# A first routed layer run ahead of the state-space scans instead of behind them, in a two-layer kernel on one core

## The reference

```python
xn = layernorm(x)
x = x + scan_block(xn) + routed_experts(xn)      # layer 0
xn = layernorm(x)
x = x + retention(xn) + two_of_sixteen(xn)       # layer 1

# scan_block: 256 inner channels, N = 16 states
Xm = silu(conv4(Xn @ W_up1));  delta = softplus(Xm @ W_ll + b)
A_bar = exp(delta * A);  U = Xm * (A_bar - 1) / (delta * A) * delta * B
H_t = A_bar_t * H_{t-1} + U_t;  y_t = sum_n C_t[n] * H_t[:, n]
out = X + (y * silu(Xn @ W_up2)) @ W_down

# routed_experts: each of 8 experts takes its 512 best tokens
G, idx = top_k(softmax(xn @ Wr).T, 512)
X_e = gelu(xn[idx] @ W1 + b1) @ W2 + b2
out = zeros.at[idx].add(G * X_e)
```

## Time and profile before

| | us |
|---|---|
| median of three runs | 572.08 |
| profiled execution | 572.04 |
| its span, first to last instruction | 570.2 |
| busy in the span: PE, DVE, ACT, POOL | 502.4, 420.6, 324.8, 370.8 |
| front, to the first scan of batch 0 | 0 to 89.0 |
| scans, to the last residual | 89.0 to 300.1 |
| experts 1 to 7, and the sums of all eight | 300.1 to 372.6 |
| second layer | 372.6 to 570.2 |

### The profile page before, as it was taken

One profiled execution on the slowest core, in us unless ns is written; L12 is line 12 of the kernel. 1 busy time (PEld: TensorE's weight loads), 2 busy tenths in 40 slices (PEclk: granted clock), 3 DMA queues, 4 the chain that ended last, 5 costly groups with the idle time before them and its releaser, 6 DMA issues.

```text
span 570.2 us, 14135 instructions
## 1 busy us (share of the span) xinstructions
PE 502.4 (88%) x4743; PEld 360.6 (63%) x4744; DVE 420.6 (74%) x1031; ACT 324.8 (57%) x787; POOL 370.8 (65%) x335
## 2 busy tenths in 40 slices
PE   0999987689999999999779999987889899999980
PEld 0643445456676777666547766544566899999970
DVE  4556549999999999999974235588767766666664
ACT  1787669567797897896133444146665544444420
POOL 5078676668898999999964776612567245455540
PEclk9899997859999999999899999998899899999995
DMA  8999631322130340414505456698111212222207
GB/s 224 171 240 294 177 113 43 128 96 101 52 151 16 151 159 7 166 23 161 187 21 159 145 181 203 189 337 327 34 48 50 62 47 61 57 54 54 57 9 221
DMA packets 58164, 70.95 MB, mean 124 GB/s; under 512 B 9343, under 2 KB 45270, under 8 KB 55168
## 3 DMA queue, kind: packets, MB, share of 16 engines
q1 hardware_dynamic: 52432, 57.84, 32.3%
q0 software_dynamic: 5392, 11.76, 8.1%
q10 hardware_dynamic: 288, 0.66, 0.5%
HBM read 50.03 MB, written 21.25 MB: 125 GB/s over the span
## 4 chain that ended last, share of the span: by engine, by line
PE 49%; POOL 18%; DVE 16%; ACT 6%; issue 5%; DMA 4%; SPq 1%; DVEq 0%; POOLq 0%; ACTq 0%
POOL arena L2064 14%; PE banks L1627 8%; PE banks L1614 8%; PE banks L1390 5%; PE banks L1250 5%; DVE arena L569 5%; POOL xm L2051 3%; PE banks L1324 3%; PE banks L1164 3%; PE banks L1174 3%; PE banks L1410 2%; PE banks L1467 2%; ACT arena L1744 2%; PE banks L1354 2%; DVE hbuf L769 1%
## 5 line engine op out<-in xcount | busy, mean ns | idle before, releaser
L2064 POOL TENSOR_TENSOR arena<-arena,bd 128x512 f32<-128x512 f32 x125 | 158.1, 1288 | 23.7 <-DVE arena L569 23.0
L569 DVE TENSOR_TENSOR_SCAN arena<-banks,arena 128x256 f32<-128x256 f32 x256 | 156.4, 669 | 3.2 <-PE banks L1164 1.3
L1744 ACT ACTIVATE arena<-delta,nega 128x256 f32<-128x256 f32 x256 | 109.5, 495 | 35.4 <-PE banks L1174 26.9
L2154 POOL DMA_INDIRECT pair_rows<-w1b,xnT x48 | 49.6, 1033 | 58.9 <-DVE w1b L858 51.8
L1627 PE MATMUL banks<-arena,hbuf 128*128 x384 | 54.7, 285 | 0.7 <-issue 0.2
L1614 PE MATMUL banks<-xsT,xm 128*128 128x128 f32 x384 | 51.1, 276 | 0.8 <-DVE acc L832 0.8
L1627 PEld LDWEIGHTS banks<-arena,hbuf 128*128 128x128 f32 x384 | 46.5, 191 | 3.6 <-issue 2.0
L1164 PE MATMUL banks<-xnT,xnw 44*128 44x172 f32 x384 | 39.9, 344 | 8.6 <-DVE arena L569 6.1
L1614 PEld LDWEIGHTS banks<-xsT,xm 128*128 128x128 f32 x384 | 46.6, 192 | 1.2 <-DVE acc L832 1.0
L2102 POOL DMA_INDIRECT expert_rows<-gate,zbuf x32 | 35.4, 1106 | 17.3 <-issue 8.8
L1830 ACT ACTIVATE hbuf<-banks,colv 128x512 f32<-128x512 f32 x32 | 22.0, 688 | 40.4 <-PE banks L1250 39.7
(11 more groups left out here) (312 smaller groups left out, 999.7 us busy)
## 6 DMA issues: line engine op xcount, KB each, us to landing
bd<-c_rows SPq DMA_DIRECT2D x16, 1024.0 KB, 6.4
expert_rows<-blank SPq DMA_DIRECT2D x8, 1024.0 KB, 10.0
xnT<-expert_rows SPq DMA_DIRECT2D x4, 1024.0 KB, 4.9
bd<-in_w SPq DMA_DIRECT2D x4, 1024.0 KB, 12.9
arena<-in_w SPq DMA_DIRECT2D x4, 1024.0 KB, 13.9
slots_in<-blank POOLq DMA_DIRECT2D x1, 3120.0 KB
xnT<-slots_in SPq DMA_DIRECT2D x48, 65.0 KB
xnw<-expert_rows SPq DMA_DIRECT2D x3, 1024.0 KB, 6.2
```

Of the source, the lines that this page charges most:

```text
L569: m = V.tensor_tensor_scan(ring[:, s, r, :], dw_view(s)[:, 2 * (s % 2) + r, :], ring[:, s, r, :], 0.0, ALU.add, ALU.mult)
L1744: m = nc.scalar.activation(ring[:, s, r, :], delta[:, half(s), bass.ds(b * L, L)], ACT.Exp, scale=negs[:, half(s), n:n + 1])
L2064: nc.gpsimd.tensor_tensor(ring[:, s, :, :], ring[:, s, :, :], c_view(par, s), ALU.mult).then_inc(S["z_pool"], 1)
L2154: nc.gpsimd.indirect_dma_start(out=yd, out_offset=bass.IndirectOffsetOnAxis(ap=xs[:, u, P:P + 1].bitcast(I32), axis=0), in_=ys[:, u % 4, : ...
```

## The change

The eight experts run in one piece between the front and the scans. Their buffers move to places that are free then: gathered rows and the transposed rows to `bd` (four experts deep), weights to `xnT` and `w1b`/`w2b` (four deep), the gated output to the upper half of `z2p`, the rows read back to the upper half of `arena` (experts 6 and 7 to the weight buffers). All eight index lists come from one-hots, with the counting row now read from SBUF. Staircases, compaction and gathers leave the batches. The preparation of the first scan batch moves from the front behind the last `up0`, and its bands go from POOL to DVE. All softplus work of ACT and DVE is done ahead of the experts' loop. The rows of experts 6 and 7 are added during batches 1 and 2, a quarter after steps 3, 5, 7 and 9. The second layer starts straight from the last residual, with 6 instead of 20 useless products, and its loads of constants go out during batch 7. Half of x is loaded by ACT, and the convolution weights wait for it.

```diff
 # DVE
-            for c in range(2): add_log(c)          # ahead of place
 def one_hot(e):
-    V.tensor_tensor(hot[e - AHEAD], iota_ps[:, None, :]..., place[:, :, e:e + 1]..., ALU.is_equal)
+    if e > 1: dve.wait_ge(S["cp_ready"], e - 1)
+    V.tensor_tensor(hot[e % 2], iota_p[:, None, :]..., place[:, :, e:e + 1]..., ALU.is_equal)
+one_hot(0); one_hot(1); indices(0); one_hot(2); indices(1)
+for c in range(2): add_log(c)
+indices(2); one_hot(3)
+for c in range(2, 6): add_log(c)
+for k in range(4): last_steps(k)
+dve_at["steps"] = link.n
+for e in range(E0):
+    if e + AHEAD < E0: indices(e + AHEAD)          # AHEAD = 3
+    if e == E0 - 1:
+        for g in range(4): band(0, 0, g)
+    gated(e)
+    if e + AHEAD + 1 < E0: one_hot(e + AHEAD + 1)
+    if e > 1: row_sum(e - 2)
 def main(b, par, last=False):
-    (batch 0: add_log and last_steps; indices at s == 1)
+    if b in (1, 2) and 2 < s < 11 and s % 2:
+        e = E0 - 3 + b
+        if s == 3: dve.wait_ge(S[f"rows_in{e % 2}"], 80); dve.wait_ge(S["dn_evac"], 1 + b)
+        sum_rows(e, (s - 3) // 2)
 for b in range(NB): main(b, b % 2, b == NB - 1)
-one_hot(5); ...; one_hot(7); expert_steps(((3, gated), (5, row_sum))); layer0_sum(q)
 # SP
+for e in range(2): weights(e)
 sp.wait_ge(S["gates_ready"], 1); (gates into token_rows)
+for e in range(2, 4): weights(e)
+sp.wait_ge(S["dve_link"], dve_at["steps"]); (b2r)
+for e in range(4): weights(e + 4); rows_in(e)
+rows_in(4); rows_in(5); c_spread(0)
+rows_in(6); c_spread(1)        # its second half now waits for ye_ready of all eight
+rows_in(7)                     # waits for row_sum 7
 for b in range(2, NB): c_spread(b)
 sp.wait_ge(S["ab_ready"], 7 * 16); (constants of layer 1)
+sp.wait_ge(S["dve_done"], 7); resident(q)
 # PE
-    (in widen, last block: pro1a(0); pro1b(0); pro2(0))
+for e in range(AHEAD): compact(e)
+turn_rows(0)
+for e in range(E0):
+    if 0 < e < E0 - 1: down0(e - 1)
+    up0(e)
+    if e + AHEAD < E0: compact(e + AHEAD)
+    if e + 1 < E0: turn_rows(e + 1)
+pro1a(0); pro1b(0); down0(E0 - 2); pro2(0); down0(E0 - 1)
 fill(0, 0, 0); fill(0, 0, 1); pro3(0)
 for b in range(NB): main(b, b % 2, b < NB - 1)
-keep_busy(12, 4 * P); pe.wait_ge(S["pair_in0"], 16); keep_busy(8, 4 * P)
+pe.wait_ge(S["dn_evac"], 10); keep_busy(6, 4 * P)
 # ACT
+for q in range(1, 4, 2): act.dma_start(acc[quarter q], x[quarter q])
+act.dma_start(wup1, w_up1); act.wait_ge(S["rows_at1"], 16); (convb)
+logarithms((6, 7)); rows_out(0); expert_steps(((2, gelus), (1, rows_out)))
+act.wait_ge(S["cp_ready"], E0); pro_a(0, 0)
 def main(b, par, more):
+    if b == 0 and s == 8: act.wait_ge(S["row_sum"], E0 - 2)
-    (stair; size_parts, size_exps and logarithms in batch 0)
 # POOL
 def gather(e, q):
+    if e > 3: pool.wait_ge(S["ye_ready"], e - 3)
-    (in main: band of batch 0, gather at chosen steps)
+for e in range(E0):
+    for q in range(4): gather(e, q)
+    if e >= AHEAD: put(e - AHEAD)
+for e in range(E0 - AHEAD, E0):
+    if e == E0 - 1: pro_c(0)
+    put(e)
+for b in range(NB): main(b, b % 2, b < NB - 1)
```

More of the change, by code:

```diff
@@ new lines, in _ @@
+            one_hot(0)
+            one_hot(1)
+            indices(0)
+            one_hot(2)
+            indices(1)
+            for c in range(2):
+                add_log(c)
+            indices(2)
+            one_hot(3)
+            for c in range(2, 6):
+                add_log(c)
+            for k in range(4):
+                last_steps(k)
+                dve.wait_ge(S["dve_link"], link.n)
+            dve_at["steps"] = link.n
+            for e in range(E0):
+                if e + AHEAD < E0:
+                    indices(e + AHEAD)
+                if e == E0 - 1:
+                    for g in range(4):
+                        band(0, 0, g)
+                gated(e)
+                if e + AHEAD + 1 < E0:
+                    one_hot(e + AHEAD + 1)
+                if e > 1:
+                    row_sum(e - 2)
@@ L1253, in main, with down0 @@
+            def down0(e):
+                pe.wait_ge(S["h_ready"], (e + 1) * HC)
+                if e > 1:
+                    pe.wait_ge(S["ye_ready"], e - 1)
+                for q in range(4):
+                    for c in range(HC):
+                        m = pe.matmul(bank[4 + e % 2][:, q * P:(q + 1) * P], hbuf[:, e % 2, c, q * P:(q + 1) * P],
+                                      w2e[e][:, c, :], start=(c == 0), stop=(c == HC - 1))
+                m.then_inc(S["d_ready"], 1)
             def main(b, par, more):
@@ L1739, in main @@
                     act.wait_ge(S["y_done"], b * 8 + (2 * (s // 4) + s % 2 + 1))
-                    if not later(b, 1) and s == 10:
-                        act.wait_ge(S["dve_link"], dve_at["logs"])
+                    if b == 0 and s == 8:
+                        act.wait_ge(S["row_sum"], E0 - 2)
                     for r in range(2):
@@ L1836, in rows_out @@
                     act.wait_ge(S["u_ready"], (e - 1) * HC)
-                nc.scalar.activation(xgT[:, e % 2, :], bank[6 if e else 7][:, :], ACT.Copy).then_inc(S["xg_sb"], 1)
+                nc.scalar.activation(xgT[:, e % 2, :], bank[6][:, :], ACT.Copy).then_inc(S["xg_sb"], 1)
             rows_out(0)
             expert_steps(((2, gelus), (1, rows_out)))
+            act.wait_ge(S["cp_ready"], E0)
+            pro_a(0, 0)
+            act.wait_ge(S["dve_link"], dve_at["steps"])
+            for b in range(NB):
+                main(b, b % 2, b < NB - 1)
             def third_norm(q):
```

449 lines of the change are left out of this document (163 added, 286 removed).

## The result

The changed kernel took **579.36 us** (median of 20 runs, 574.06 to 583.21), the kernel before 574.54 (20 runs on the same chips, 571.31 to 580.92). The ratio is **1.0079, 95% interval 1.0051 to 1.0106**: slower by 0.5 to 1.1%. The profiled execution took 577.68 us, 575.8 of it span, against 572.04 and 570.2; that pair differs by 5.6 us, a little more than the medians (4.8).

A forecast was written before the change was run, and what follows sets the result against it. DVE was taken to pace the batches, with the experts a PE pipeline behind them. Experts and front reach the first scan at 188.0; scans 190.7, seam 3.5, then 5.6, 190.6 and 1.84 give 580.2 us; range 574 to 587.

The forecast's parts named there:

- seam: Between scans and second layer: half the last sum, finish, down, residual and handovers take 3.5 us; before it was 10.
- the rest: From the second layer's first transposition to the end of the span: stays at 190.6 us.
- Blocking: In the experts: POOL's indirect copies wait for the end of one-hots with two SBUF inputs, 3.9 and 6.8 us.
- The first rival: In the experts: one-hots do not block POOL's copies, 3.9 and 5.8 us go, 570.5 us, no change; chance 0.23.
- POOL ends last in the experts: At the last gathered rows: POOL, not PE, ends last by 5.8 us; without the blocking, even with PE.
- DVE sets the pace of the scans: In the scan batches: DVE, not POOL, is the bound; batches 3 to 6 take 91.1 us.
- The second rival: In the scans: POOL is the bound, so leaving gathers save 22 us instead of about 5: 563 us; chance 0.07.
- Row sums: In batches 1 and 2: four DVE additions of expert rows each, at 0.85 us, 3.4 us per batch.
- Batch 7: Last scan batch: 27.22 us less an index list, a wait and 2.1 of three slowed products, 24.0 us.
- The front: From the start to `tokp`: 88.95 us falls by 4.8 to 84.15.
- The load of x: At the start: half of x on the other queue lets DVE start earlier, 1.3 us less (bounds 0 and 2.5).
- The third rival: In the experts: PE's clock falls in pauses waiting for the last gathers, costing 5 us: 586 us; chance 0.14.

The follow-up runs named there:

- counter_psum: The changed kernel with the eight one-hots reading their counter from PSUM instead of SBUF; ratio to the kernel before 0.9938, median 571.15 us.
- before_counter_sbuf: The kernel before with the counter of its three DVE one-hots in SBUF instead of PSUM, nothing else; one execution, 572.85 us.
- sums_on_pool: The changed kernel with the eight row sums of experts 6 and 7 on POOL, in batches 1, 2, 4 and 5; ratio to the kernel before 0.9953.

## Why the prediction was right

The direction and the mechanism held, and the sum missed the profiled execution by 2.5 us and the median (579.36) by 0.8. Its steps, with what the trace has in their place:

| step | predicted | measured |
|---|---|---|
| `tokp` | 84.15 | 82.83 |
| `tokp` to first gather | 5.05 | 5.67 |
| first gather to first transposition | 11.2 | 9.09 |
| fourth index list | 110.3 | 105.6 |
| PE's wait for the last rows | 5.8 | 5.64 |
| last transposition ends | 167.2 | 163.3 |
| first scan of batch 0 | 188.0 | 184.69 |
| scans | 190.7 | 188.68 |
| seam | 3.5 | 3.97 |
| to the first transposition of the second layer | 5.6 | 5.89 |
| the rest | 190.6 | 192.57 |

That the time came so near is in part luck. Up to the end of the scans the trace is 5.3 us ahead of the sum, because most steps were priced too dear; 2.8 us come back behind that, 2.0 of them with the 16 products at the lower clock level. And the sum counts from an execution of 572.04, while the kernel before took 574.54 in the twenty runs beside the changed one. The change itself was forecast at 8.2 us and measured at 4.8 (medians) or 5.6 (the profiled pair). Its ratio, 1.0079, lies within the 1% that the prediction set as the bound of "same", to which it gave 0.29; only by the time, 579.36 against a bound of 577.8, is it "slower".

**Blocking** (the cost that the diff does not show) is what decided it. The steps priced it at 3.9 + 6.8 = 10.7 us on POOL; the long copies show 2.6 + 5.9 = 8.4, and `counter_psum` took it away with one operand: ratio 1.0079 to 0.9938. The first rival (no blocking) is out by that. The forecast puts 9.7 us between itself and that rival; `counter_psum` shows 6.0 of the way, and 8.2 between the medians. So the term was somewhat too dear, and that the rival's 570.5 is nearly the time of the kernel with the cause removed (571.15 the median, 572.13 the profiled execution) owes something to the other steps. The size was taken from rows of 1.25 and 1.49 us beside operations of 1.35 and 2.49. These are two rows with the delay, not the three that the prediction counts, and the copy does not end when DVE ends: the first ends 0.86 us behind the product (291.53 against 290.67), as the six do behind the one-hots. The first miss of the term is `one_hot(2)`, which began 0.95 us ahead of the first gather instead of together with it, and so cost 1.35 and not 2.2.

The Trainium skill, "SBUF — State Buffer", section "Who interferes with whom", had a sentence for each side. The trace agrees with the first (a DVE instruction with two SBUF inputs holds up a GpSimd instruction that reads SBUF, for its whole length): copies of 2.88 and 2.95 us behind one-hots that began 0.25 and 0.18 earlier. The second, that a `tensor_tensor` was not seen to stall the writing of descriptors, gives no safety here, since these one-hots are `tensor_tensor` operations. Whether an indirect copy is held when it reads its index list from SBUF, as the first sentence would have it, or when descriptors are written, no run here separates. The same section says that issue order decides who blocks; the copy at 298.95 in `before_counter_sbuf`, 0.05 us ahead of the one-hot and undelayed, agrees. The one-hot that began inside that copy took its 2.29 us too, so in this order neither was held.

**POOL ends last in the experts**: the waits of PE, 5.64 against 5.8, are there, for experts 5 to 7 rather than 6 and 7. That the two figures are so near is chance: without PE's 3.0 us of slower work the waits would have been about 8.7 (an estimate from the rows of PE above). What the step left out is the loop the other way: without blocking, POOL waits for the index list that PE makes late, 1.29 us in `counter_psum`.

**DVE sets the pace of the scans.** Batches 3 to 6: 91.09 us against 91.1. The second rival (POOL) is out by that and by `sums_on_pool`. Row sums were priced at 0.85, measured 0.67. Batch 7 took 22.5, not 24.0; DVE's three products there took 0.67 to 0.70 us against 1.35 to 2.73. 1.35 + 1.56 + 2.73 less three times 0.69 is 3.6 us that went, and the step had taken 2.1. What had held them is not a gather. In the kernel before each began inside POOL's own products with C and ended 0.55 or 0.56 us behind them:

```profile
272.43 2.49 POOL L2064 TENSOR_TENSOR arena<-arena,bd 128x512 f32<-128x512 f32 x2
272.75 2.73 DVE L518 TENSOR_TENSOR arena<-arena,bd 128x512 f32<-128x512 f32 x1
...
287.60 2.51 POOL L2064 TENSOR_TENSOR arena<-arena,bd 128x512 f32<-128x512 f32 x2
```

The second pair is completed by DVE's product at 289.32 in the earlier trace rows. In the kernel after POOL no longer lags, and the order can turn round; here DVE's product is first, and POOL's takes 1.63 us instead of 1.27:

```profile
359.96 0.67 DVE L506 TENSOR_TENSOR arena<-arena,bd 128x512 f32<-128x512 f32 x1
360.12 1.63 POOL L1988 TENSOR_TENSOR arena<-arena,bd 128x512 f32<-128x512 f32 x1 [0.99 <-DVE arena L615]
```

**The front** came out 1.3 us better than its step in this execution. Over the eight profiled executions with the new front the median of `tokp` is 84.5 us, near the step's 84.15, so the 82.83 is an early one. The load of x, priced at 1.3 and bounded by 2.5, starts DVE 2.7 us earlier and is worth nothing that the runs show. So most of the gain, 6.1 us here, would come from batch 0's preparation leaving the search, priced at 3.5; that was not tried by itself and is not shown.

**The third rival** (the clock falls in PE's pauses) came in part, and not as it was told. Its sign, `up0` of experts 6 and 7 at twice its duration, is absent (3.60 and 3.67 us); `down0` was slower instead. That is 3.0 us of work, where the rival took 5, and up to the last transposition it only shortened PE's waits. Where such work lies behind the last wait, as `up0` of 5.37 us does in `counter_psum`, no wait for rows follows that could take it up.

## What to carry to other kernels

Before moving work ahead of a hidden stage, list what hid it: here the scans had covered compaction, the way in and most of the gathers, and the experts took 28.6 us more without that cover (6 of them by the blocking), against 25 won elsewhere. When a long VectorE operation with two SBUF inputs is put beside a run of indirect DMAs on GpSimd, move one input to PSUM: one operand was worth 1.4% here. A chain of waits names the engine that came last, not the one with no slack: a stage's bound shows in the stretches, and is tested by moving work onto the engine that the chain names.

## What was not expected of the hardware

An indirect copy held up by a one-hot ends 0.81 to 0.96 us after it, in all six cases of the kernel after; one that began 0.05 us before the one-hot ran undisturbed in 0.94 us. A DVE product of two SBUF tiles, 0.67 us alone, took 1.35 to 2.73 where it began inside POOL's products of two SBUF tiles in the kernel before, and a POOL product that began inside DVE's took 1.63 instead of 1.27, so between such products the hold works both ways. And TensorE's lower clock level is not a matter of the kernel alone: the same 16 products of the second layer took 2.02 us (granted clock 1.00) or 3.75 (0.50) from one execution to another, in kernels of either kind, and moved the end by about 2 us.
